# Softmax maxima in four two-bank reductions per period, and another cut of the value products

## The reference

```
scores  = einsum('blhd,bshd->bhls', q, k) / sqrt(16)
weights = softmax(scores, axis=-1)
out     = einsum('bhls,bshd->blhd', weights, v)
```

## Time and profile before

| | us |
|---|---|
| runs of the kernel before | 3443.15, 3441.13, 3438.78 |
| median | 3441.13 |
| profiled execution, first to last instruction (its span) | 3437.2 |

### The profile page before, as it was taken

How to read it: one execution, slowest core, us unless ns; L and a number is a source line. 1 busy time by engine, 2 the same in 40 slices (tenths; PEclk the granted TensorE clock), 3 DMA queues, 4 the chain that set the end, 5 groups by cost and what they waited for, 6 DMA issues and landing times. The chain is left out here.

```text
span 3437.2 us, 66173 instructions
## 1 busy us (share of the span) xinstructions
PE 3289.5 (96%) x25137; PEld 1521.3 (44%) x25138; DVE 2955.9 (86%) x4695; ACT 2473.5 (72%) x4700; POOL 580.5 (17%) x601
## 2 busy tenths in 40 slices
PE   8999999999999999888899889999999999999997
PEld 5433333333333333567677656533333333333332
DVE  8889999999999997353787665499999999999991
ACT  4178888888888888533333324688888888888886
POOL 4410000000000000053331143133333210000001
PEclk9689999999999999889999999999999999999999
DMA  8451220202021100345010376513132231202001
GB/s 270 138 140 47 41 39 15 44 16 39 15 44 32 24 15 5 129 135 191 27 36 12 121 248 200 139 35 58 35 52 45 52 64 27 44 16 40 15 16 49
DMA packets 306934, 232.77 MB, mean 68 GB/s; under 512 B 205591, under 2 KB 257720, under 8 KB 301970
## 3 DMA queue, kind: packets, MB, share of 16 engines
q1 hardware_dynamic: 290308, 179.45, 22.6%
q0 software_dynamic: 14832, 47.79, 4.3%
q10 hardware_dynamic: 1504, 1.64, 0.1%
HBM read 126.49 MB, written 102.76 MB: 67 GB/s over the span
## 5 line engine op out<-in xcount | busy, mean ns | idle before, releaser
L957 ACT ACTIVATE att_l_probs<-att_l_s_ps 128x512 f32<-128x512 f32 x4096 | 2142.0, 599 | 309.5 <-PE att_l_s_ps L900 269.3
L981 DVE TENSOR_REDUCE att_in_part_max<-att_l_max_ps 128x1 f32<-128x512 f32 (+1 forms) x2928 | 2292.0, 885 | 9.9 <-PE att_l_max_ps L890 9.5
L915 PE MATMUL att_l_o_ps<-att_l_probs,att_l_v_sb 128*17 128x512 f32 (+2 forms) x11776 | 1171.5, 470 | 1.4 <-DMA att_l_v_sb<-v_rows 1.1
L900 PE MATMUL att_l_s_ps<-att_in_q_sb,att_in_k_sb 50*128 50x512 f32 x2048 | 734.4, 453 | 10.1 <-DVE att_l_o_ps L995 9.0
L900 PE MATMUL att_l_s_ps<-att_in_q_sb,att_l_k_sb 50*128 50x512 f32 x2048 | 727.0, 453 | 1.3
L890 PE MATMUL att_l_max_ps<-att_l_k_sb,att_in_q_sb 50*128 50x512 f32 x2048 | 722.4, 445 | 5.2 <-DVE att_in_part_max L981 5.2
L890 PE MATMUL att_l_max_ps<-att_in_k_sb,att_in_q_sb 50*128 50x512 f32 x1856 | 660.0, 449 | 5.0 <-DVE att_in_part_max L981 4.8
L890 PEld LDWEIGHTS att_l_max_ps<-att_l_k_sb,att_in_q_sb 50*128 50x128 f32 x2048 | 336.2, 184 | 319.7 <-DVE att_in_part_max L981 297.8
L900 PEld LDWEIGHTS att_l_s_ps<-att_in_q_sb,att_l_k_sb 50*128 50x128 f32 x2048 | 328.6, 184 | 267.5 <-ACT att_l_probs L957 238.4
L900 PEld LDWEIGHTS att_l_s_ps<-att_in_q_sb,att_in_k_sb 50*128 50x128 f32 x2048 | 335.1, 186 | 241.3 <-ACT att_l_probs L957 202.3
L890 PEld LDWEIGHTS att_l_max_ps<-att_in_k_sb,att_in_q_sb 50*128 50x128 f32 x1856 | 307.8, 186 | 290.5 <-DVE att_in_part_max L981 268.4
(11 more groups left out here) (264 smaller groups left out, 2758.3 us busy)
## 6 DMA issues: line engine op xcount, KB each, us to landing
att_in_q_sb<-q_hi SPq DMA_DIRECT2D x256, 64.0 KB
slot_rows<-att_l_zeros POOLq DMA_DIRECT2D x10, 1024.0 KB, 4.5
ffn_parts<-slot_rows SPq DMA_DIRECT2D x40, 256.0 KB, 3.1
tile_out<-ffn_parts SPq DMA_DIRECT2D x40, 256.0 KB, 2.2
att_in_q_sb<-q_lo SPq DMA_DIRECT2D x128, 72.0 KB
att_l_v_sb<-v_rows SPq DMA_DIRECT2D x16, 544.0 KB, 15.2
att_in_k_sb<-k_hi SPq DMA_DIRECT2D x32, 256.0 KB, 8.9
att_l_k_sb<-k_hi SPq DMA_DIRECT2D x32, 256.0 KB, 9.4
```

The costliest lines, as they stand in the source:

```text
L900: nc.tensor.matmul(s_ps[:, c % SB], k_sb[j // GPB % 2][rows, pair, u * P:(u + 1) * P], q_sb[rows, j % QR, pair], start=True, stop=True).th ...
L915: last = nc.tensor.matmul(o_ps[32 * h:32 * h + AUG, c0:c1], v_sb[:, j // GPB % 2, u, h * AUG:(h + 1) * AUG], probs[:, (n * KT + u) % PB, h ...
L957: nc.scalar.activation(probs[:, (n * KT + u) % PB, h], s_ps[:, c % SB], ACT.Exp, scale=float(HD) ** -0.5).then_inc(exp_done, 1)
L981: nc.vector.reduce_max(dst, banks, AX.X).then_inc(units_taken, 1)
```

## The change

There are four takes in a period, units (0, 1), (2, 3), (4, 5) and (6, 7), each one instruction over two neighbouring banks that writes two neighbouring maxima. To make them neighbours the order of the two halves is swapped in `part_max`, in the first maxima of an attention, and where the shift rows are stored.

The order of PE becomes

```diff
--- before.py
+++ after.py
@@ -254,7 +254,7 @@
         pair, tile, part = maximum_parts(k % MAXI)
         for half in range(2):
             rows = slice(half * HROWS, half * HROWS + XROWS)
-            last = nc.tensor.matmul(ps[:, k % 2 * 2 + half], ai.q[rows, j, pair, tile * P:(tile + 1) * P],
+            last = nc.tensor.matmul(ps[:, k % 2 * 2 + 1 - half], ai.q[rows, j, pair, tile * P:(tile + 1) * P],
                                     ai.k[0][rows, pair, part * G:(part + 1) * G], start=True, stop=True)
         last.then_inc(ai.slot_ready, 1)
         beside(k)
@@ -299,7 +299,7 @@
             row = half * HROWS + SHIFT0 + part
             dst = ai.q[:].bitcast(F32)[row:row + 1, j % QR].rearrange("r p (t b i) -> r (p t) b i", b=P // CUTS, i=CUTS)
             src = io.shift.rearrange("(b r h c) i -> r h c b i", r=NSHIFT, h=2, c=PAIRS * TPG)
-            eng.dma_start(dst, src[part:part + 1, half]).then_inc(ai.shift_stored, 16)
+            eng.dma_start(dst, src[part:part + 1, 1 - half]).then_inc(ai.shift_stored, 16)
 
 
 def heads_of(dram):
@@ -635,9 +635,9 @@
 STEPS_G = KT // STEP_TILES
 UNITS = 4 * STEP_TILES
 MB = 4
-TAKES = ((0,), (1, 2), (3,), (4,), (5, 6), (7,))
+TAKES = ((0, 1), (2, 3), (4, 5), (6, 7))
 TAKE_OF = {i: t for t, units in enumerate(TAKES) for i in units}
-ROUNDS = ((3, 0, 288), (2, 288, 512), (3, 0, 512))
+ROUNDS = ((2, 1, 0, 256), (2, 1, 256, 512), (4, 0, 0, 512))
 RESULT_STEP, ROWMAX_STEP = 1, LEAD // STEP_TILES
 DIVIDE_STEP, PARTS_STEP, ZERO_GROUP = RESULT_STEP + 1, ROWMAX_STEP, 1
 
@@ -935,18 +935,16 @@
             pe.wait_ge(o_zeroed, 1)
             for n in range(STEPS):
                 for w in range(STEPS_G):
-                    if w == 0:
-                        products(n, w, 0, 3)
-                        if n > 0:
-                            values(n - 1, KT - 1, 0, G)
-                        products(n, w, 3, 5)
-                        values(n, 0, 0, G)
-                        continue
                     pair = 0
-                    for r, (count, c0, c1) in enumerate(ROUNDS):
+                    for count, back, c0, c1 in ROUNDS:
                         products(n, w, pair, count)
                         pair += count
-                        values(n, STEP_TILES * w - (r < 2), c0, c1)
+                        if w > 0:
+                            values(n, STEP_TILES * w - back, c0, c1)
+                        elif back and n > 0:
+                            values(n - 1, KT - 1, c0, c1)
+                        elif c1 == G and not back:
+                            values(n, 0, 0, G)
             values(STEPS - 1, KT - 1, 0, G)
 
         @block.scalar
@@ -974,8 +972,8 @@
                 if p >= PERIODS:
                     return
                 g, k, half = unit_of(n, w, units[0])
-                first = 2 * k + half
-                dst = part_max[:, g % 2, first:first + 1] if len(units) == 1 else part_max[:, g % 2, first:first + 4:3]
+                first = 2 * k + 1 - half
+                dst = part_max[:, g % 2, first:first + len(units)]
                 banks = max_ps[:, units[0] % MB:units[0] % MB + len(units)]
                 dve.wait_ge(unit_ready, UNITS * p + units[-1] + 1)
                 nc.vector.reduce_max(dst, banks, AX.X).then_inc(units_taken, 1)
```

## The result

The changed kernel takes 3605.86 us (median of four runs, 3605.12 to 3609.57), the kernel before 3439.95 beside it: a ratio of 1.0482 [1.0467, 1.0497]. That is 166 more, 7 under the forecast of 3613.

A forecast was written before the change was run, and what follows sets the result against it. DVE was taken to set the period, 4.77, with PE close behind. The new period of 5.11 gave +166 over 488 periods, plus 6.5 for 24 without units: +172, a median of 3613, range 3525 to 3650.

The forecast's parts named there:

- The step that carries it: Pairs p4 to p7: with three score banks, p7's score load waits for p4's exponential and comes 1.25 after p4's load.
- The group of four: PE's run of pairs p4 to p7 with no block of values between: forecast to take 1.68 instead of 1.15.
- The bank wait beside it: p6's maximum load, about 0.85 after p4's, waits for the double over units 2 and 3; alone it makes the group 1.53.
- rival 3: Only the banks hold p4 to p7: group 1.53, period 4.96, +97, 3538; needs p4's exponential 0.15 earlier; chance 0.06.
- the 24 periods without units: Periods without maximum products, 12 in each attention: same ACT chain, 4.88 for 4.61, +6.5 together.
- The prices: PE's costs without waits: each 256 block 0.555, two pairs 0.67, a further pair 0.24, the 512 block's stretch 0.98.
- PE's 4.58 without waits: Sum of PE's own work over one period of the new order, if no load waits: 4.58.
- The transpose's thin cover: Result transpose behind take 1: take 2 released at 3.83, next p0 load at 3.885; cover gone costs at most 38.
- the 3.9 between span and median: Kernel before: runs' median 3441.13 stands 3.9 above the profiled span 3437.2; carried along unchanged into the forecast.
- Rival 1: DVE stays the bound, as p7 does not wait: period falls by 0.11, 3441 - 54 = 3387; chance 0.06.
- Rival 2: Gain and wait cancel, the run p4 to p7 near 1.34, time within 0.2% of before; chance 0.03.
- rival 4: Waits add up: p4's exponential queues for one more, or the transpose's cover goes; 38 to 250 more, 3651 to 3863; chance 0.05.

The follow-up runs named there:

- the short exponentials: Changed kernel with each exponential over 128 of the 512 queries, the other probabilities set to 1 once per attention: 3521.9 us, 1.024 of the kernel before.
- the two kernels with POOL's reciprocal: Kernel before with the row sums' reciprocal moved from DVE to POOL: 3442.12 us; the same with DVE's reciprocal kept in each attention's last step: 3438.05 us.

## Why the prediction was right

**The step that carries it**, that p7's score waits for p4's exponential because no block stands between them any more, is shown: p7's load is 1.24 after p4's (forecast 1.25), and the time follows the length of the exponential, over three lengths, and not that of the takes. The group of four took 1.68, as forecast.

**The bank wait beside it** came as worked out, 0.83 (0.85) with DVE named, and costs nothing beside the longer one; alone it gives 4.91 in most periods and 4.94 on average, for which I had 4.95 or 4.96. This is rival 3, and what it needed, an earlier exponential, is what the short exponentials gave it: 3521.9 for its 3538, with the 24 periods without units shorter too (4.30 for 4.87, about 14 us, which rival 3 did not have).

**The prices.** Blocks of 256 0.55 to 0.56 (0.555), groups of two 0.66 (0.67), the period 5.09 (5.11); the periods without units 4.87 (4.88), by the starts of the exponentials in the last step. That last one is luck: 4.88 was the middle between two bounds 0.46 apart, and no row decided for it. PE's 4.58 without waits was not seen in any run.

**DVE.** Its gaps were forecast at about 0.5 and show as 0.24. The row of four takes is also longer than four unbroken ones would be, 4.79 for 3 x 1.13 + 1.21 = 4.60: its first takes start 1.22 apart, at the pace of PE's groups, and as a record lasts 1.22 no gap shows between them. So part of the free time hides in a row that looks busy, and the prediction's sentence that a full DVE row can't hide waiting is wrong: one has to look at the distance of the starts. This changes nothing in the time. The transpose's thin cover held: the step is eight equal periods.

**Where the 7 us are.** Span against span the sum had 172 more, and the profiled executions show 170.6 (3607.8 for 3437.2). Most of the 7 is the 3.9 between span and median that I carried along: it was spread among executions. Here a run's time lies 1.8 above its own span (3609.57 for 3607.8), and the profiled execution is the slowest of the four. Within the 170.6, the two attentions, from first to last exponential, grew by 79.2 and 84.8, together 164; the 0.02 of the period makes 488 x 0.02 = 10 of difference to the 172. Against that stands the first step of the second attention, 3.6 more than the other steps explain: TensorE's clock, for which I had charged nothing, was low in it for longer (last section). The other 6.6 lie between the attentions, a stretch whose code didn't change: it took 797.4 for 790.8 in the profiled executions, and 790.8 to 801.2 over all kernels of this study, one execution each: spread that no sum could foresee. That the sums agree so closely is thus in part luck.

**The rivals.** Rival 1 fell: p7 waits, and with DVE's reductions cut to half this order still takes 3602.89. Rival 2 fell with the group's 1.68, rival 4 since ACT was idle before p4 (0.19 in front of its exponential at 850.38). The rule of the Trainium skill (Perfetto Trace Analysis, Optimizing Scalar/DVE Operations) on larger operations would have put the time at rival 1; with the takes alone the larger reductions cost 265. Its other advice, to break instructions up, holds by its words where the engine is not saturated but causes bubbles on others, a condition that the prediction left out. It fits one pair of runs here, the order of before with four takes (3705.72) and with six (3440.43), and not the other, the new order with four (3605.86) and with six (3684.36); DVE had gaps in both kernels with four.

## What to carry to other kernels

Before work is moved so as to relieve a full engine, cut that engine's work short and run it: here the order of before gave back some 46, with PE and ACT right behind DVE. Work that stands between two uses of the same buffers hides a round trip; where it is moved, price the round trip (here load to load 1.24 over three score banks) against what is left between, and cut or merge consumers only along the groups of the producer, since a merged consumer holds its buffers until its last part is there. Where two waits run side by side, taking one away wins only the difference, so both must be named and priced.

## What the runs showed of the hardware that I had not expected

The second attention opens with TensorE at the lower of its two levels, 1.2 GHz. In both kernels PE had worked 0.83 us of the 5 us before and the granted clock of the first period is 0.50. But in the changed kernel the second period, the third row of windows above, still stands at 0.50 and takes 8.45; in the kernel before the clock rose within it (a mean of 0.83):

```profile
2203.62:2209.18 5.56, 5.56 (x44) 2.00 (x42) 4.95 (x7) 4.24 (x9) 0.96 (x1) 0.83 1.04 124
```

So the first step of that attention took 46.19 for 39.99, 6.2 more, where other steps grew by 2.57. The change need not be the cause: of the two kernels with POOL's reciprocal, which both open the attention with the order of before, one took 5.17 for that period at a mean of 0.90, the other 8.17 at 0.50. Why the clock comes up later in some executions was not tried.

Half of a change can cost more than the whole: here the order alone costs 244, the takes alone 265, both together 166.

POOL's power over 128x16 took 2.92, twelve times DVE's reciprocal of the same tile.
